# A transformer block on one core: maxima by tiles of 64 query rows, exps in pairs, products in the rings

## What is computed

```python
qkv = x @ w_attn + b_attn                       # 16 heads of 8 channels
att = einsum('bhqd,bhkd->bhqk', q, k) * scale   # 512 x 512 for each head
att = softmax(where(causal, att, -inf))
y = einsum('bhqk,bhkd->bhqd', att, v) @ w_proj + b_proj
x1 = layernorm(x + y)
xr, xk = mixes of x1 with x1 shifted by one position (mu_r, mu_k)
r = sigmoid(xr @ W_r.T);  k = square(relu(xk @ W_k.T))
out = layernorm(x1 + r * (k @ W_v.T))
```

## Time and profile before

| | |
|---|---|
| median of 3 runs | 318.31 us |
| the profiled execution's own time | 318.81 us |
| its span, first to last instruction | 317.1 us |
| mean granted clock of TensorE | 0.956 of full |
| PE busy | 279.0 us (88%) |
| DVE busy | 276.1 us (87%) |
| ACT busy | 252.4 us (80%) |
| POOL busy | 223.5 us (70%) |

### The profile page before, as it was taken

One profiled execution on the slowest core, in us unless ns is written; L12 is line 12 of the kernel. 1 busy time (PEld: TensorE's weight loads), 2 busy tenths in 40 slices (PEclk: granted clock), 3 DMA queues, 4 the chain that ended last, 5 costly groups with the idle time before them and its releaser, 6 DMA issues.

```text
span 317.1 us, 7851 instructions
## 1 busy us (share of the span) xinstructions
PE 279.0 (88%) x2449; PEld 119.7 (38%) x2450; DVE 276.1 (87%) x1236; ACT 252.4 (80%) x504; POOL 223.5 (70%) x426
## 2 busy tenths in 40 slices
PE   7289878999999999999899989998999898897971
PEld 3113323344343534443345335433534334333341
DVE  5599789999999999999999999999999999961475
ACT  2323886799978999999999999999989897797550
POOL 5520573668776889688968898688868897587722
PEclk9755999999999999999999999999999999997997
DMA  2361341134112510252125212341035101110011
GB/s 87 98 156 34 77 127 38 34 89 119 37 36 51 135 35 26 73 136 69 35 69 138 69 36 67 80 130 37 1 104 132 41 3 35 36 35 1 2 33 34
DMA packets 32939, 20.43 MB, mean 64 GB/s; under 512 B 7297, under 2 KB 32898, under 8 KB 32898
## 3 DMA queue, kind: packets, MB, share of 16 engines
q1 hardware_dynamic: 31394, 19.08, 22.6%
q10 hardware_dynamic: 1504, 0.85, 1.1%
HBM read 4.72 MB, written 2.10 MB: 22 GB/s over the span
## 4 chain that ended last, share of the span: by engine, by line
PE 46%; DVE 32%; ACT 6%; issue 6%; POOL 5%; DMA 2%; SPq 2%; POOLq 0%; DVEq 0%; ACTq 0%
DVE masked L881 22%; PE pv_ps L541 14%; PE sh_ps L473 9%; PE ex_ps L525 9%; PE sh_ps L479 7%; PE mx_ps L510 4%; DVE stats L916 3%; ACT probs L704 2%; POOL probs L1124 2%; ACT vals L740 1%; PE sh_ps L466 1%; DVE y_rows L899 1%; SPq L342 1%; DVE m_max L881 1%; DMA b_row<-in_L_attn_b_attn_dram 1%
## 5 line engine op out<-in xcount | busy, mean ns | idle before, releaser
L881 DVE CUSTOM_DVE_ANT_0 masked<-mx_ps,mask_wide 128x384 f32<-128x384 f32 (+3 forms) x512 | 216.6, 483 | 12.9 <-PE mx_ps L510 12.6
L704 ACT ACTIVATE probs<-ex_ps 128x512 f32<-128x512 f32 x320 | 174.8, 608 | 20.8 <-PE ex_ps L525 18.2
L510 PE MATMUL mx_ps<-k_st,q_st 64*128 64x384 bf16 (+3 forms) x512 | 106.7, 311 | 13.6 <-DMA k_st<-k_part 6.0
L525 PE MATMUL ex_ps<-q_st,k_st 64*128 64x128 bf16 (+3 forms) x512 | 99.3, 302 | 6.4 <-DMA q_st<-m_turn 4.2
L1124 POOL TENSOR_SCALAR_AFFINE_SELECT probs<-probs 128x512 f32<-128x512 f32 x128 | 79.4, 638 | 21.0 <-ACT probs L704 20.9
L541 PE MATMUL pv_ps<-probs,vals 128*32 128x512 f32 (+3 forms) x1024 | 89.2, 444 | 2.4 <-DVE y_rows L899 1.6
L525 PEld LDWEIGHTS ex_ps<-q_st,k_st 64*128 64x128 bf16 x512 | 34.5, 94 | 84.6 <-ACT probs L704 55.9
L510 PEld LDWEIGHTS mx_ps<-k_st,q_st 64*128 64x128 bf16 x512 | 33.6, 94 | 37.9 <-DVE m_max L881 25.1
L881 DVE DVE_READ_ACCUMULATOR2_ANT m_max<- 128x1 f32 x512 | 43.5, 85 | 0.0
L541 PEld LDWEIGHTS pv_ps<-probs,vals 128*32 128x32 f32 x1024 | 22.4, 108 | 24.3 <-issue 18.1
L1200 POOL TENSOR_TENSOR mixT<-mix_cur,mix_prev 128x512 f32<-128x512 f32 x14 | 17.8, 1272 | 1.6 <-ACT mix_prev L760 1.6
(11 more groups left out here) (147 smaller groups left out, 337.3 us busy)
## 6 DMA issues: line engine op xcount, KB each, us to landing
q_st<-q_part SPq DMA_DIRECT2D x42, 128.0 KB
k_st<-k_part SPq DMA_DIRECT2D x42, 128.0 KB, 2.4
x_in<-in_L_attn_x_dram SPq DMA_DIRECT2D x8, 256.0 KB, 2.9
q_st<-m_turn SPq DMA_DIRECT2D x128, 2.0 KB
x_res<-in_L_attn_x_dram SPq DMA_DIRECT2D x8, 256.0 KB, 2.9
out_dram<-o_sb SPq DMA_DIRECT2D x7, 256.0 KB, 2.4
q_st<-q_part SPq DMA_DIRECT2D x4, 96.0 KB
k_st<-k_part SPq DMA_DIRECT2D x4, 96.0 KB, 3.0
```

The costliest lines, as they stand in the source:

```text
L510: last = mm(ps[:, at:at + n], q_st[b % 2][side, slot, t * P:(t + 1) * P], k_st[b % 2][side, slot, 0:n], start=True, stop=True)
L525: last = mm(ps[:, at:at + n], k_st[b % 2][side, slot, t * P:(t + 1) * P], q_st[b % 2][side, slot, t * P:T], start=True, stop=True)
L704: act.activation(dst, src, ACT.Exp, scale=SCALE).then_inc(exp_done, 1)
L881: last = dve.tensor_tensor_reduce(out=masked[unit % len(masked)][:, at:at + n], in0=mx_ps[unit % MX_BANKS][:, at:at + n], in1=mask_wide[:, ...
```

## The change

The maxima are taken by tiles of 64 query rows. Two heads of one side stand above one another: head 0 on partitions 0 to 63 of the bank, head 1 on 64 to 127, each by a matmul with 64 stationary columns. There are 8 such tiles of 64, 128, ... 512 keys for each side, so a group has 2 x 2304 = 4608 columns for DVE where it had 4 x 1280 = 5120; the number of DVE instructions stays at 16 a group. A unit is now tile 7, or 6 and 0, or 5 and 1, or 4 and 2, or 3 (256 columns only), of one side. The logits are computed with keys in halves of 64, two matmuls beside one another where there was one, and in pairs of units: 1024 columns over two banks, which ACT takes with one instruction. `ex_ps` becomes two such pairs of banks.

`sh_ps` is gone. `proj` and `kv`, which DVE reads, are entries in the ring of `mx_ps`; the other seven products are entries in the ring of `ex_ps`, each holding a pair. The tables for PE, and for the steps of ACT and DVE that read a product, become one table `RING_AT`; the others have new numbers. The values products of a group are issued two by two. In the head POOL instead of ACT makes the middle parts, SP and ACT issue the stacking DMAs in another order, SP and ACT share the four row DMAs of group 0, and POOL builds the masks and widens the bias. In the last sequence `residual` on POOL moves from before the mixes (20; mixes at 23 and 24) to behind them (24; mixes at 19).

```diff
--- before
+++ after
-MX_FILLS = fills((3,), (2, 0), 1, 1)
+HALF_ROWS = P // SIDES
+TILES = T // HALF_ROWS
+MX_FILLS = [(s, tiles) for tiles in ((7,), (6, 0), (5, 1), (4, 2), (3,)) for s in (1, 0)]
...
-PV_UNITS = (1, 5, 7, 7)
+PV_UNITS = (0, 0, 4, 4)
...
-PE_AT = {'xT': 1, 'q': 4, 'k': 8, 'v': 11, 'proj': 13, 'x1T': 24, 'kT': 32, 'r': 35, 'kv': 39}
+RING_AT = {'xT': 4, 'q': 6, 'k': 7, 'v': 14, 'proj': 7, 'x1T': 28, 'kT': 33, 'r': 37, 'kv': 38}
-MX_BANKS, EX_BANKS = 3, 3
+MX_BANKS, EX_PAIRS = 3, 2
...
+READ_BY_VECTOR = ("proj", "kv")
...
+def ring_entries():
+
+    ex, mx = {}, {}
+    for unit in range(LEAD):
+        mx[unit] = len(mx)
+    for unit in range(UNITS):
+        b, at = divmod(unit, PER_SEQ)
+        if unit % 2 == 0:
+            ex[unit // 2] = len(ex)
+        if unit + LEAD < UNITS:
+            mx[unit + LEAD] = len(mx)
+        for name in RING_NAMES:
+            missing = b == 0 if name in ("proj", "x1T", "kT", "r", "kv") else b == NB - 1
+            if due("RING", name, unit) and not missing:
+                ring = mx if name in READ_BY_VECTOR else ex
+                ring[b, name] = len(ring)
+    return ex, mx
...
-        m_max = [sb(f"m_max{i}", [P, HG, NT]) for i in range(2)]
+        m_max = [sb(f"m_max{i}", [P, SIDES, TILES]) for i in range(2)]
...
-        ex_ps = [bank_of(f"ex_ps{i}") for i in range(EX_BANKS)]
+        ex_ps = [ctx.enter_context(nc.psum_tensor(f"ex_ps{i}", [P, 2 * T], F32)) for i in range(EX_PAIRS)]
         pv_ps = bank_of("pv_ps")
-        sh_ps = bank_of("sh_ps")
+        ex_bank = [ex_ps[i // 2][:, i % 2 * T:i % 2 * T + T] for i in range(2 * EX_PAIRS)]
...
+        def product_bank(name, b):
+
+            if name in READ_BY_VECTOR:
+                return mx_ps[MX_ENTRIES[b, name] % MX_BANKS]
+            return ex_ps[EX_ENTRIES[b, name] % EX_PAIRS][:, 0:T]
...
-                for a in range(ROW_DMAS):
-                    sp.dma_start(rows[:, :, a, :], m_turn[group % 2][a * 32:(a + 1) * 32, :]).then_inc(rows_stacked, 16)
+                if group == 0:
+                    stack_rows(sp, group, range(ROW_DMAS // 2))
+                else:
+                    stack_rows(sp, group, range(ROW_DMAS))
...
             first_slots(sp, 0, 0)
-            first_slots(sp, 1, 0)
             first_slots(sp, 0, 2)
+            first_slots(sp, 1, 1)
             first_slots(sp, 1, 2)
...
+            def acquire(name, b):
+
+                if name in READ_BY_VECTOR:
+                    wait(pe, mx_read, MX_ENTRIES[b, name] - MX_BANKS + 1)
+                else:
+                    wait(pe, ex_read, EX_ENTRIES[b, name] - EX_PAIRS + 1)
+                return product_bank(name, b)
...
-                wait(pe, mx_read, unit - MX_BANKS + 1)
-                ps, at = mx_ps[unit % MX_BANKS], 0
-                for h, t in MX_FILLS[u][1]:
-                    n, (side, slot) = (t + 1) * P, side_of(group % SLOTS, h)
-                    last = mm(ps[:, at:at + n], q_st[b % 2][side, slot, t * P:(t + 1) * P], k_st[b % 2][side, slot, 0:n],
-                              start=True, stop=True)
+                entry = MX_ENTRIES[unit]
+                wait(pe, mx_read, entry - MX_BANKS + 1)
+                ps, at = mx_ps[entry % MX_BANKS], 0
+                s, tiles = MX_FILLS[u]
+                for t in tiles:
+                    n, queries = (t + 1) * HALF_ROWS, slice(t * HALF_ROWS, (t + 1) * HALF_ROWS)
+                    for i in range(HG // SIDES):
+                        side, slot = side_of(group % SLOTS, s * (HG // SIDES) + i)
+                        last = mm(ps[i * HALF_ROWS:(i + 1) * HALF_ROWS, at:at + n], q_st[b % 2][side, slot, queries],
+                                  k_st[b % 2][side, slot, 0:n], start=True, stop=True)
                     at += n
                 last.then_inc(mx_full, 1)
 
-            def logits(unit):
-
-                b, group, u = place(unit)
+            def logits(pair):
+
+                b, group, u = place(2 * pair)
                 if u == 0:
                     wait(pe, rows_stacked, (group + 1) * ROWS_STACKED)
 
-                wait(pe, exp_done, unit - EX_BANKS + 1)
-                ps, at = ex_ps[unit % EX_BANKS], 0
-                for h, t in EX_FILLS[u][1]:
+                entry = EX_ENTRIES[pair]
+                wait(pe, ex_read, entry - EX_PAIRS + 1)
+                ps, at = ex_ps[entry % EX_PAIRS], 0
+                for h, t in EX_FILLS[u][1] + EX_FILLS[u + 1][1]:
                     n, (side, slot) = T - t * P, side_of(group % SLOTS, h)
-                    last = mm(ps[:, at:at + n], k_st[b % 2][side, slot, t * P:(t + 1) * P], q_st[b % 2][side, slot, t * P:T],
-                              start=True, stop=True)
+                    for i in range(P // HALF_ROWS):
+                        keys = slice(t * P + i * HALF_ROWS, t * P + (i + 1) * HALF_ROWS)
+                        last = mm(ps[i * HALF_ROWS:(i + 1) * HALF_ROWS, at:at + n], k_st[b % 2][side, slot, keys],
+                                  q_st[b % 2][side, slot, t * P:T], start=True, stop=True)
                     at += n
                 last.then_inc(ex_full, 1)
...
-                wait(act, ex_full, unit + 1)
-                src = ex_ps[unit % EX_BANKS][:, :]
+                entry = EX_ENTRIES[pair]
+                wait(act, ex_full, entry + 1)
                 (h, t), *more = EX_FILLS[u][1]
                 if (h + 1, t) in more:
-                    src = src.rearrange("p (h q) -> p h q", h=2)
-                    dst = probs[group % 2][:, h:h + 2, PCOL[t]:PCOL[t] + T - t * P]
+                    src = ex_ps[entry % EX_PAIRS][:, :].rearrange("p (h q) -> p h q", h=HG)
+                    dst = probs[group % 2][:, :, PCOL[t]:PCOL[t] + T - t * P]
                 else:
-                    dst = probs[group % 2][:, h, PCOL[t]:PCOL[t] + T]
-                act.activation(dst, src, ACT.Exp, scale=SCALE).then_inc(exp_done, 1)
+                    src = ex_ps[entry % EX_PAIRS][:, :].rearrange("p (s q) -> p s q", s=SIDES)
+                    dst = probs[group % 2][:, h:h + HG // 2 + 1:HG // 2, PCOL[t]:PCOL[t] + T]
+                act.activation(dst, src, ACT.Exp, scale=SCALE).then_inc(ex_read, 1)
...
-            mids(0, -1, 0)
-            mids(1, -1, 0)
+            first_slots(act, 1, 0)
             first_slots(act, 0, 1)
-            first_slots(act, 1, 1)
...
+            stack_rows(act, 0, range(ROW_DMAS // 2, ROW_DMAS))
...
-                for h, t in MX_FILLS[u][1]:
-                    n = (t + 1) * P
+                s, tiles = MX_FILLS[u]
+                for t in tiles:
+                    n = (t + 1) * HALF_ROWS
                     last = dve.tensor_tensor_reduce(
-                        out=masked[unit % len(masked)][:, at:at + n], in0=mx_ps[unit % MX_BANKS][:, at:at + n],
+                        out=masked[unit % len(masked)][:, at:at + n], in0=mx_ps[entry % MX_BANKS][:, at:at + n],
                         in1=mask_wide[:, T - n:T], op0=ALU.add, op1=ALU.max, scale=1.0, scalar=LOWEST,
-                        accum_out=m_max[group % 2][:, h, t:t + 1])
+                        accum_out=m_max[group % 2][:, s, t:t + 1])
...
+            for i in range(2):
+                _, part, _, rest = q_and_k[i]
+                pool.wait_ge(rest_done[i], 1)
+                pool.tensor_copy(part[:, 1, :], rest[:, :]).then_inc(mid[i], 1)
```

More of the change, by code:

```diff
@@ L99 @@
+TABLES = {"RING": (RING_AT, LAST_RING_AT), "ACT": (ACT_AT, LAST_ACT_AT), "DVE": (DVE_AT, LAST_DVE_AT),
           "POOL": (POOL_AT, LAST_POOL_AT), "SP": (SP_AT, LAST_SP_AT)}
@@ L348, in other_slots, with stack_rows @@
             stack_piece(eng, which, part, range(FIRST_SLOTS, STACKED), (q_stacked, k_stacked)[which])
+        def stack_rows(eng, group, quarters):
+            b, g = divmod(group, SLOTS)
+            wait(eng, m_turned, group + 1)
+            for a in quarters:
+                i, part = divmod(a, ROW_DMAS // PAIRS)
+                rows = q_st[b % 2][MAX_BAND::MAX_STEP, PAIRS * g + i, :].rearrange("j (t a r) -> j t a r", t=TILES, r=32)
+                eng.dma_start(rows[:, :, part, :], m_turn[group % 2][a * 32:(a + 1) * 32, :]).then_inc(rows_stacked, 16)
         def stack_part(eng, which, part, b):
@@ L579, in _ @@
                 for t in half_tiles(half):
[L580 removed]
+                    last = pe.transpose(ex_bank[half][:, t * P:(t + 1) * P], x_in[0][:, t, :], ident[:, :])
                 last.then_inc(x_turned[half], 1)
@@ L589, in _ @@
                 mm(mx_ps[i][:, :], w[:, :], xT[:, :], start=True, stop=True).then_inc(first_full[i], 1)
-            values(-1)
+            for t in range(NT):
+                last = mm(ex_bank[2][:, t * P:(t + 1) * P], xT[:, t * P:(t + 1) * P], w_in[:, 2 * C:3 * C], start=True, stop=True)
+            last.then_inc(head_full, 1)
             pe.wait_ge(ones_stacked[0], 16)
@@ L1121, in zero_behind @@
                 after = dict(ZERO_AFTER)[t]
-                wait(pool, exp_done, group * EX_UNITS + after)
```

(1 more changed line is left out.)

261 lines of the change are left out of this document (135 added, 126 removed).

## The result

The changed kernel takes 329.78 us (median of 4 runs, 328.56 to 333.90), the kernel before 318.32 us beside it on the same chip: ratio 1.036, 95% interval 1.032 to 1.040. It is slower by 11.5 us. The forecast was 305.4 us with a range of 295 to 327: wrong in sign, and the time lies outside the range.

The account below looks back on a forecast made before the run. PE, DVE and ACT, all within 7% of the 33.84 us period, were taken to bound it together. A 32.36 us period saves 10.4 us over seven, head 1.3, tail 1.2: 305.4 us on the median's scale, range 295 to 327.

Parts of the forecast that it names:

- Ring waits: Two-entry exps ring shared with seven products: waits cost 0.3 us a period on the path, bounds 0 and 2.6.
- rival 3: Waits in the ring of two eat the gain, leaving only part of head and tail: 317 us, chance 0.10.
- The sum: Whole kernel: period gains of 10.4 us, head 1.3 and tail 1.2 off 318.8 give 305.9, or 305.4 as median.
- Seams: PE insertions between logits and maxima: four fewer a sequence at 0.27 us each, 0.67 us a period on the path.
- Maxima, DVE: 512 fewer columns a group save DVE 2.06 us a period, 0.83 of it on the path.
- DVE stage: First 12.96 us of a sequence, DVE busy throughout: 0.40 of DVE's work in a period, where its savings count.
- Maxima and logits, PE: Doubled matmuls cost 10 ns each, 0.79 us a period in PE's stage; fewer columns give 0.26 back.
- The shared bank: From v to the projection PE waits for ACT's two copies of the values; removing this saves 0.81 us a period.
- Exps in pairs: A pair takes ACT 0.91 us; ACT gains 1.2 us a period, counted as nothing on the path.
- Head: Start of the kernel: shared row DMAs and shorter first maxima, less 0.3 us for POOL's copies, give -1.3 us.
- Tail: Last sequence: `residual` moves behind the mix, taking 1.24 us off the chain, counted as -1.2 us.
- what is late next: After the shared bank goes, the turning of y for the projection, due three DVE units earlier, is late; no price.

Follow-up runs that it names:

- e6: Changed kernel with single exps in a ring of four banks and the tables and values' places of the kernel before: 316.89 us, ratio 0.9958.
- e3: Changed kernel with the tables and values' places of the kernel before; pairs, rings and tiles as changed: 333.44 us, ratio 1.0509.
- e15: e6 with three banks instead of four in the ring of exps, the fourth unused: 338.31 us, ratio 1.0626.
- e10: e6 with each product in the ring of exps holding two of the four banks: 338.43 us, ratio 1.0649.
- e9: e6 with PE issuing the logits of two units together, ACT still taking and returning single banks: 331.64 us, ratio 1.0411.
- e5: Changed kernel with single exps in a ring of four banks, new tables kept: 340.34 us, ratio 1.0692.
- e13: e6 with the values of key tiles 0 and 1 together at unit 5: 332.07 us, ratio 1.0447.
- e14: e6 with the values of key tiles 1, 3 and 2 together at unit 7: 323.01 us, ratio 1.0154.
- e17: e6 with the values of the four key tiles each at its own unit (1, 3, 5, 7): 335.60 us, ratio 1.0518.
- e18: e6 with the values of key tile 0 at unit 3 instead of 1: 335.92 us, ratio 1.0554.
- e4: Changed kernel with the values of key tile 1 at unit 2 instead of 0: 336.55 us, ratio 1.0615.
- e2: Kernel before with doubled matmuls and maxima by tiles of 64 rows; shared bank, single exps and old tables kept: 316.97 us, ratio 1.0000.
- e1: Kernel before with each matmul of maxima and logits issued as two with 64 stationary columns: 318.45 us, ratio 1.0036.
- e8: e2 with the projection and kv in the ring of maxima, the other seven products in the shared bank: 317.34 us, ratio 0.9989.
- e7: Changed kernel with SP's table of the kernel before, stacking of q and k five units later: 326.82 us, ratio 1.0187.
- e12: e6 with the last sequence's residual on POOL behind the mixes, unit 26 instead of 20: 317.58 us, ratio 0.9981.

## Why the prediction was wrong

**Ring waits, the step that failed.** "I take 0.3 us a period on the path; bounds 0 and 2.6 (all the gains above)." At the old places the pairs cost 2.1 us a period (e6 against e3), in all 16.5 us, and e15 and e10 reach 21 with one bank less or one bank more held. The argument against rival 3, that a pair holds as much work as two of three banks, counted what ACT has in front of it. It left out how long PE is held, and what stands behind in its list. Two ways show. Where a product takes half of the ring (e10), PE waits before the next logits for ACT's second read, and maxima that have a free bank stand behind. Where two units of logits stand together (e9), PE must get through two units of maxima before it can give ACT more, and it waits for DVE's banks there. Rival 3 named the first; e3 and the changed kernel show mainly the second (PE's loads wait 42.3 and 52.3 us for DVE's maxima, 21.6 and 6.9 for ACT's exps). Its price was bounded by the gains, which excluded a result above 318.8 from it; no row gave that bound. A bound for a coarser ring must come from how long PE is held, not from what the change is to win.

**The new places, valued as gains alone.** The sum has the new numbers of the tables as -0.67 us a period for seams and -0.81 for the projection, and nothing against them but the 0.3 of the ring waits. Without the pairs they cost 23.5 us (e6 to e5), so they lose more than the pairs do by themselves; together with the pairs the loss is 12.9 (e6 to the changed kernel). The two don't add up, and either part can be called the cause by the order in which they are undone. The traces differ: from e6 to e3 PE's idle time grows from 36.0 to 48.3 us and its busy time by 4.5; from e6 to e5 its idle grows to 44.7 and its busy time by 17.5; in the changed kernel they are 40.2 idle and 9.4 more busy. So the rings show mostly as idle of PE, the places mostly as longer work of PE. Why that work gets longer no run shows; that the two sides overlap less and that the granted clock is lower would both fit.

**Seams.** "A seam costs 0.27 us", four fewer: -0.67 us a period. The durations were right: values of tiles 0 and 1 together take 1.64 to 1.71 us in place of two stretches. But merging alone costs 15 and 6 us (e13, e14). That a longer stretch without logits or maxima empties both rings would explain these two, not e17 and e18. With pairs it is otherwise: there (0, 2, 4, 4) instead of (0, 0, 4, 4) costs 6.8 us (e4; 8.1 by the ratios). What places these stretches well stays open, as e17 and e18 show: the old numbers are the best of those tried for single banks (e5, the new numbers with single banks, 23.5 us above e6), the new ones suit pairs better (e3 to the change: 3.7 us, 4.7 by the ratios), and by what rule no run says.

**Maxima, DVE.** "2.06 us a period", 0.83 on the path. The instructions came as worked out (673 ns for 512 columns, 421 for 256, 219 for 64), and DVE's busy time fell by 11.6 us in the change and by 15.1 in e2. On the path this gave at most the 1.1 us that the doubled matmuls cost (e1, e2). "DVE stage", a stretch in which DVE had no idle, was read as a bound; PE was busy 11.83 of its 12.96 us, so PE was next at once.

**Maxima and logits, PE.** "I take 10 ns" for each added matmul with its load: e1 gives 1 ns. In the changed kernel the loads overlap (timeline of the weight loads):

```profile
152.41 0.33 PEld L573 LDWEIGHTS ex_ps<-q_st,k_st 64*64 64x64 bf16 x8
```

eight loads of 107 ns within 0.33 us. A pair of logits and two maxima took 0.77 us at 152.38, not 0.6. By the rule of the Trainium skill (TensorEngine Tiling (Array Packing), Restrictions and Gotchas) that column tiling excludes Fast Weight Load these loads go without it. The trace does not speak against it, as a load of 64 columns takes no less than one of 128 did before (107 ns, 94 before), but no run shows the reason; e1 shows that it costs nothing that matters here. The halves do run together, as taken.

**The shared bank.** "0.81 us a period". The wait was smaller than that. PE itself stood for ACT's copies 2.2 us in the whole kernel before, 0.4 at most:

```profile
PE sh_ps L473 <- ACT vals L740: 2.2, 6, 0.4
```

The 0.81 was the copies' own time on the chain, in which PE had other work for the most part. e8 takes the wait away alone and gains nothing. Seen the other way, the bank is worth 21 us as an entry: with the seven products in a ring of three and no bank for them the time is 338.31 (e15), with the fourth 316.89 (e6).

**Exps in pairs.** ACT's instruction takes 1022 ns and comes every 0.92 us back to back, 0.91 estimated. ACT was busy 9.4 us less, as estimated (1.2 a period), and waited 16.9 longer.

**SP's queue.** Not in the prediction: some 5 us (e7).

**Head, -1.3 us.** The first logits of group 0 start at 27.60 us, before at 27.49. The chain after (start, us, what):

```profile
17.70 4.08 DMA mu<-in_L_ffn_mu_k_dram
...
21.90 0.29 POOL b_v_wide L1316
...
23.41 1.34 ACTq L382
...
24.79 2.68 DMA q_st<-m_turn
```

The row DMAs are issued from 23.41 us instead of 24.02 and land at 27.47; before, the logits started at 27.49. So nothing is won. The split of the maxima now stands on POOL behind the widening of the bias, which waits for a load. "POOL's copies" had a price in the prediction; the other work that the change puts on POOL in the head had none.

**Tail, -1.2 us.** With e12 the residual's move gives nothing. In the last sequence something else costs: the granted clock, in windows of the changed kernel. A shorter fall, which the kernel before does not have, stands first; another like it begins at 80 us.

```profile
53.00:57.00 4.00, 3.74 (x26) 0.91 (x30) 2.52 (x15) 1.02 (x1) 1.06 (x2) 0.57 0.00 0
...
274.00:278.00 4.00, 2.78 (x54) 1.47 (x46) 3.78 (x14) 2.96 (x3) 2.11 (x6) 1.00 0.18 51
278.00:282.00 4.00, 3.09 (x30) 2.39 (x26) 3.09 (x15) 0.00 (x0) 3.54 (x11) 0.56 0.26 69
282.00:286.00 4.00, 4.00 (x36) 1.34 (x36) 3.11 (x18) 2.70 (x4) 2.48 (x10) 0.58 0.00 1
```

PE is idle 1.2 of the 4 us from 274, two waits for DVE's maxima, and 0.9 of the next, in which the projection waits for the turned y ("what is late next", as the prediction had it, without a price). Then the clock stands near its lower level of 1.2 GHz: the chain there shows

```profile
279.03 2.08 PE mx_ps L514 x8
...
283.10 2.76 PE pv_ps L591 x16
```

for a projection that takes 1.14 at full clock and values of 1.71: 2 us together. The 4.5 us behind the last add are for the most part not this, but the units that now stand there. Over the span the clock takes at most (1 - 0.931) x 326.9 = 22.6 us, against (1 - 0.956) x 317.1 = 14.0 before, an estimate that counts PE as never idle. These 8.6 us are nearly the whole 9.8 us by which the span grew, so how much of the loss is the clock and how much waiting stays open. It is not all: the period from 141.51 us, at 1.00, is 1.05 us longer than before, and e3, e10 and e15 are slower than the changed kernel at 0.958, 0.964 and 0.970.

**The sum.** From e6 to the changed kernel by way of e3: +16.5 for the pairs, -3.7 for the new numbers in all tables, which hold SP's 5 against them. By way of e5: +23.5 for the new numbers, -10.6 for the pairs. From before to e6, with tiles, doubled matmuls and rings: -1.4 us, where the forecast's steps for the same parts were to give 9 (7 x 1.11, and the head's 1.3).

## What to carry to other kernels

Before a ring is made coarser, work out for its producer how long it is held at each entry, foreign entries included, and what else stands in its list behind that wait: here a late reader of one ring starved the reader of the other. Where three engines are within 7% of the period, a saving on one becomes its idle, and the chain that the profile shows is one of several: try each part alone. A table of places is fitted to the ring that it was made with: undo a part under both the old and the new numbers (here the pairs cost 16.5 us under the one and gained 10.6 under the other), and look at every queue in which the table moves DMAs.
